# Layer two's features in another order, and four gathered quads instead of one ahead of the score block

## What is computed

```python
Qh = (x @ Wq + bq).reshape(N, 8, 32); Kh = (x @ Wk + bk)...; Vh = (x @ Wv + bv)...
s = jnp.einsum('nhc,nhc->nh', Qh, Kh) / jnp.sqrt(32.)      # one score a node and head
alpha = jax.nn.leaky_relu(s[src] + s[dst], 0.2)
m = jax.ops.segment_max(alpha, dst, num_segments=N)
e = jnp.exp(alpha - m[dst])
attn = jax.ops.segment_sum(Vh[src] * (e / denom[dst])[:, :, None], dst, num_segments=N)
```

## Time and profile before

| | |
|---|---|
| median of 3 runs | 2749.72 us (2741.72 to 2752.97) |
| the profiled execution's own time | 2740.57 us |
| its span | 2738.8 us |
| PE, DVE, ACT, POOL busy | 61%, 60%, 30%, 53% |
| mean granted clock of PE | 0.802 of full speed |

### The profile page before, as it was taken

How to read it: one execution, slowest core, us unless ns; L and a number is a source line. 1 busy time by engine, 2 the same in 40 slices (tenths; PEclk the granted TensorE clock), 3 DMA queues, 4 the chain that set the end, 5 groups by cost and what they waited for, 6 DMA issues and landing times. The chain is left out here.

```text
span 2738.8 us, 38544 instructions
## 1 busy us (share of the span) xinstructions
PE 1679.5 (61%) x9983; PEld 1342.2 (49%) x9983; DVE 1652.3 (60%) x2687; ACT 833.9 (30%) x2134; POOL 1444.6 (53%) x1557
## 2 busy tenths in 40 slices
PE   4367534677655544486655777504477767767688
PEld 4255423455543433486544566403355545545577
DVE  6455763677654545676424655796366657668675
ACT  3144210000000000465212222205355545534454
POOL 3655676655656664526155555477665655530050
PEclk8599857788876776588777999856689888878899
DMA  4535544555423333344152545454555555331010
GB/s 137 183 101 159 178 140 123 170 174 157 120 81 92 95 92 106 112 142 131 51 175 81 163 154 160 161 190 128 157 166 170 172 164 158 106 101 32 4 43 31
DMA packets 132988, 346.47 MB, mean 127 GB/s; under 512 B 39881, under 2 KB 66521, under 8 KB 119347
## 3 DMA queue, kind: packets, MB, share of 16 engines
q0 software_dynamic: 66144, 180.94, 23.5%
q1 hardware_dynamic: 63407, 158.51, 16.5%
q10 hardware_dynamic: 3364, 6.16, 0.7%
HBM read 262.24 MB, written 83.28 MB: 126 GB/s over the span
## 5 line engine op out<-in xcount | busy, mean ns | idle before, releaser
L1366 PE MATMUL ms_ps_m<-ms_msg,ms_pick 128*128 128x260 f32 x1408 | 415.6, 458 | 287.1 <-issue 199.8
L892 POOL DMA_INDIRECT e_ring<-table,e_index x465 | 442.6, 952 | 252.2 <-issue 137.6
L1347 DVE TENSOR_TENSOR ms_msg<-e_ring,ms_ps_w 128x1040 f32<-128x1040 f32 (+1 forms) x352 | 436.6, 1240 | 141.8 <-issue 128.0
L1366 PEld LDWEIGHTS ms_ps_m<-ms_msg,ms_pick 128*128 128x128 f32 x1408 | 313.0, 229 | 389.7 <-issue 332.2
L1366 PE MATMUL ms_ps_m<-ms_msg,all_xn 128*128 128x272 f32 x1408 | 386.0, 437 | 191.5 <-issue 167.1
L892 POOL DMA_INDIRECT e_ring<-table,l_index x369 | 353.9, 959 | 227.3 <-issue 111.1
L1366 PEld LDWEIGHTS ms_ps_m<-ms_msg,all_xn 128*128 128x128 f32 x1408 | 290.0, 212 | 287.3 <-issue 218.9
L767 PE MATMUL sc_ps_e<-sc_keys,sc_hot 125*128 125x100 bf16 (+1 forms) x3840 | 322.7, 241 | 168.6 <-DVE all_xn L712 141.7
L767 PEld LDWEIGHTS sc_ps_e<-sc_keys,sc_hot 125*128 125x128 bf16 x3840 | 276.8, 104 | 238.8 <-issue 123.4
L934 POOL DMA_INDIRECT w_staged<-table,l_stage_index x256 | 257.3, 1005 | 183.5 <-issue 66.9
L670 ACT ACTIVATE sc_rows<-sc_ps_b 125x512 bf16<-125x512 f32 x320 | 171.2, 598 | 433.6 <-PE sc_ps_b L755 251.8
(11 more groups left out here) (513 smaller groups left out, 2743.3 us busy)
## 6 DMA issues: line engine op xcount, KB each, us to landing
ahead<-w_staged SPq DMA_DIRECT2D x32, 1056.0 KB
e_ring<-ahead SPq DMA_DIRECT2D x32, 1056.0 KB
ahead<-e_ring SPq DMA_DIRECT2D x20, 1040.0 KB
e_ring<-ahead SPq DMA_DIRECT2D x20, 1040.0 KB
e_ring<-table,e_index POOLq DMA_INDIRECT x465
all_acc<-ahead SPq DMA_DIRECT2D x27, 256.0 KB
ahead<-all_acc SPq DMA_DIRECT2D x27, 256.0 KB
e_ring<-table,l_index POOLq DMA_INDIRECT x369
```

The source lines that it names most:

```text
L892: pool.indirect_dma_start(out=g.ring[:, slot * QUAD + i // GT, i % GT, :], out_offset=None, in_=s.table[:, :], in_offset=bass.IndirectOffs ...
L1347: dve.tensor_tensor(msg[:, b, :, 0:R].rearrange("p t (h o) -> p t h o", h=H), ring[:, bass.ds(slot, 1), :, :].rearrange("p a t (h o) -> p ...
L1366: mm = pe.matmul(ps_m[b][:, 0:W], pick[:, b, t, :], msg[:, b, t, :], start=t == 0, stop=t == GT - 1)
```

## The change

`BEGUN` becomes STAGES, so POOL gathers all four quads of the first round, 32 gathers, at the end of the features' block. And the features are written in another order on PE, ACT and DVE: the values of all five blocks come before the queries and keys of blocks 1 to 4.

```diff
-    BEGUN = 1
+    BEGUN = STAGES
...
                 turn_rows(0)
                 turn_rows(1)
                 values(0)
+                turn_rows(2)
                 values(1)
+                values(2)
                 queries_and_keys(0)
-                turn_rows(2)
-                values(2)
-                queries_and_keys(1)
-                node_scores(0)
                 turn_rows(3)
                 values(3)
-                queries_and_keys(2)
-                node_scores(1)
                 turn_rows(4)
                 values(4)
-                queries_and_keys(3)
-                node_scores(2)
-                queries_and_keys(4)
-                node_scores(3)
-                node_scores(4)
+                for b in range(1, NB):
+                    queries_and_keys(b)
+                    node_scores(b - 1)
+                node_scores(NB - 1)
...
                 highs(1)
+                highs(2)
+                second_norm(3)
                 queries(0)
-                highs(2)
-                queries(1)
-                second_norm(3)
                 highs(3)
                 second_norm(4)
-                queries(2)
                 highs(4)
-                queries(3)
-                queries(4)
+                for b in range(1, NB):
+                    queries(b)
...
+                norm(1)
                 lows(0)
-                norm(1)
                 norm(2)
                 lows(1)
                 dve.wait_ge(ones_set, 1)
                 values(0)
                 values(1)
-                products(0)
                 lows(2)
-                values(2)
                 combine(3)
                 norm(3)
-                products(1)
-                keep_scores(0)
+                values(2)
+                products(0)
                 combine(4)
                 norm(4)
                 lows(3)
                 values(3)
-                products(2)
-                keep_scores(1)
                 lows(4)
                 values(4)
-                products(3)
-                keep_scores(2)
-                products(4)
-                keep_scores(3)
-                keep_scores(4)
+                products(1)
+                for b in range(NB):
+                    keep_scores(b)
+                    if b + 2 < NB:
+                        products(b + 2)
```

## The result

| | before | after |
|---|---|---|
| median (7 runs each) | 2749.72 us | 2779.72 us (2762.64 to 2789.55) |
| ratio, 95% interval | | 1.0107 (1.0073 to 1.0142) |
| the profiled execution | 2740.57 us | 2762.64 us |
| its span | 2738.8 us | 2760.9 us |
| POOL's first gather to the last score kept | 15.5 us | 60.9 us |

The stages add up: 39.2 + 5.2 - 22.6 + 1.9 - 1.5 = 22.2 us, the difference of the spans. About 6.5 of the 39.2 are older than the edit: the first value of the features is kept at 1321.08, at 1314.59 before.

The account below looks back on a forecast made before the run. No engine is busy over 61%, so waits bind, with 40.7 us lost around the score block's start. Boundary +8 and score block -24 sum to -16: 2749.7 - 16 = 2733.7 us, range 2714 to 2760.

Parts of the forecast that it names:

- Part 1, the order: Features: with values ahead of queries and keys, the last values come 12 us earlier, bounds 0 and 14.8 us.
- the 4 us for PE's lower clock level: Features: 4 us added to the hand-made chain of values for PE's lower clock level after its pauses.
- Part 2, POOL and the boundary (+8): End of the features: 30 us of gathers, less 10 of idle and 12 of earlier start, move the boundary +8 us.
- POOL has some 10 us to spare there: Ahead of the boundary: POOL's 10.56 us of idle after the first quad counted as room for gathers.
- stays within 3 us of 1392: End of the features: PE's total work is unchanged, so the last score hardly moves and doesn't hold the boundary.
- The second rival: Stops move into the features: 26 us, 8 hidden behind POOL's end, boundary 18 us later, 2751 us; chance 0.20.
- The first quad's 10 us run beside the same work cost under 2 us: Features: argument against stops moving there, from the one quad gathered beside the same work before.
- The stores at the boundary: Boundary: SP's four stores begin together beside the first loads of sc_pair; costed at 0, bound 3 us.
- Part 3, the score block (-24): Start of the score block: 16.5 us remain of 40.7 lost, a gain of 24 us, bounds 0 and 38.
- Part 4, the rest (0): From item 5 on: POOL is paced by the lookups, its head start buys nothing, all behind moves equally.
- 0.66 us per us of run: Score block: loss charged per us of POOL's unbroken indirect transfers, from 40.7 us lost over 61.5 us of runs.
- my counterexample: Weights' stage: in a 93 us run of POOL, PE's result of 1782.48 reaches DVE at 1782.79, without delay.

Follow-up runs that it names:

- e2: The changed kernel with one quad instead of four gathered ahead of the boundary, the new order of the features kept; ratio 1.0032.
- e6: The changed kernel with SP's four stores started only when the first two pair loads have landed; ratio 0.9977.
- long jobs: The three jobs in which the kernel before had a median of 2745 to 2758 us, as in the first measurement.
- short jobs: The three jobs in which the kernel before had a median of 2313 to 2316 us and no engine stood behind POOL's runs.
- f2: The kernel before with POOL waiting for one more item after every second scatter and, from the 20th on, per four gathers; ratio 1.0037.
- f3: The changed kernel with quads paced by products, scatters paced by two and SP's stores behind the first pair loads; ratio 0.9957.
- h1: The changed kernel with direct transfers of fixed rows in place of the staged quads' gathers, in one of the long jobs; ratio 0.9273.
- g2: The changed kernel, unedited, measured a third time, in one of the short jobs; ratio 1.0046.
- f1: The changed kernel, unedited, measured again in one of the long jobs; ratio 0.9971.
- e3: The changed kernel with memsets on POOL in place of 21 of the 24 gathers of quads 1 to 3 ahead of the boundary; ratio 0.9963.
- g1: The changed kernel with direct transfers of fixed rows in place of the staged quads' gathers, in one of the short jobs; ratio 0.9693.

## Why the prediction was wrong

I forecast -16 us; the profiles give +22, and 2779.7 lies above the range's 2760.

*Part 1, the order:* right. From the first value kept to the last, 1321.08 to 1365.46 is 44.4 us, where it was 1314.59 to 1371.70, 57.1: 12.7 us less, and I had said 12. All profiles agree: 42.6 to 45.7 us in the new order, 57.1 to 59.2 in the old. No row priced the 4 us for PE's lower clock level in that sum. The new order by itself leaves the last score where it was, too: 76.8 us behind the first value in e2, 77.3 before.

*Part 2, POOL and the boundary (+8):* **the step that failed**, twice over. First, "POOL has some 10 us to spare there": it had not. The 10.56 us of idle in the earlier trace rows were mostly the close of its block, which ends 8.4 to 10.2 us after the start of the last gather in every kernel here; in the kernel before it ran until 1393.65, 3.0 us ahead of the first work behind the boundary (1396.69), and where it is what binds, that distance is 1.2. So the slack was 1.8 us. I took a wait that the view named after SP for slack. With the close counted, part 2 is about +17, not +8: in the changed kernel POOL's close ended at 1419.27 and alone would have put the boundary at 1420.5. Second, the last score "stays within 3 us of 1392. It doesn't bind": it was kept at 1431.1 and it was what bound. The second rival named this mechanism, at 26 us of stops and 0.20. It was 60.9 - 26.9 = 34 us. I had 8 us of it hidden behind POOL's end; since the close is longer, some 18 were, and 1435.9 - 1420.5 = 15.4 us showed at the boundary. "The first quad's 10 us run beside the same work cost under 2 us" was true (e2: 0) and misled me: eight gathers in a row cost 0, 16 cost 12, 32 cost 29 to 34.

The stores at the boundary, "I cost it at 0, the bound is 3 us": the first reduction came 5.2 us later than before, and holding the stores back gives 9 (e6). The bound rested on a wrong reading: POOL's first transfer behind the boundary takes 2.49 us in e6 too, at 1191.60, when the first store is issued only at 1196.59. Its 2.42 us in the earlier trace rows say nothing of the store.

*Part 3, the score block (-24):* right in size: 22.6 us from the first reduction to the eleventh, 34.3 left of 56.9. The distance of the eleventh from the boundary was 56.5 us, between the "about 50" and the "over 60" that I had given.

*Part 4, the rest (0):* right in the long jobs, where 64 gathers are left to POOL behind the lookups with one quad ahead as with four, and the part behind them took 983.7 and 982.2 us.

*From -16 to +22:* 9.3 for the close (17.3 instead of 8), 15.4 for the stops behind it, 5.2 for the stores, 1.4 for part 3 (22.6 of 24), 0.4 behind the eleventh reduction, and 6.5 that are older than the edit: 38.2 us.

The reason behind part 3 was too narrow. I priced the stops at 0.66 us per us of run over a steady pace of 1.91 us a step and took that pace for PE's. In the short jobs it is 1.37 (204.0 / 149): the steady pace holds stops too. Over 218 us, the lookups lose 0.55 to 0.67 us for each of 177 to 194 indirect transfers in ten profiles, paced or not (before 123 / 194 = 0.64, after 102 / 177 = 0.58, f2 0.62, f3 0.57). So it is nearer to a toll on each transfer than to a price of long runs, and a transfer moved from one place with dense exchange between PE, ACT and DVE to another takes its toll along. It is not one price: h1's 17 transfers, nearly back to back, cost 17 us (235.0 - 218), 1.0 each. In the features the 24 moved gathers put off the last score by 34 us, 1.4 each, and the boundary by as much (31.7 us behind the first gather in e2, 65.7 here); by g2's 50.2, some 18 of these would be there without any stop, as POOL's own run and close. Leaving the score block the gathers gave back about 21 (341.4 - 320.6). That is the change. The weights' stage, with few signals, pays nothing: from the last reduction to the first work on messages it is 124.3 us before and 124.2 in g2. That was my counterexample, and it was the place to look at.

How sure is the sign? The changed kernel gave 1.0107, 0.9971 and, in a short job, 1.0046. The two in long jobs exclude each other's intervals, so jobs differ by more than the interval says; I would say between no change and 1% slower, with no run that shows a gain clear of noise. In f1 the boundary came at 1421.7 instead of 1435.9, with POOL's start 9 us earlier, which the features' first value brought along, and 29 us of stops instead of 34: that is 14 of the 25.7 us between the two spans.

## What to carry to other kernels

Work that an engine has left over beside a chain of short exchanges need not be free for the chain, even if their busy times fit: price it by an experiment that leaves the engine busy and takes away the transfers (e3, h1). Before counting an idle stretch ahead of a block's end as slack, ask what closes the block. And where several stores are made ready at once, look at what loads stand beside them: one wait on SP gave 9 us at that place, in all six runs that had it (12.9 to 13.1 us to the first reduction).

## What the runs showed of the hardware

- In the long jobs PE's, ACT's and DVE's signals come late while POOL issues indirect transfers (gathers of 135 KB as well as scatters of 4 KB), PE's up to 29 us; not while it fills memory (e3), and not with direct transfers of the same bytes (h1). I can't say what is shared. The Trainium skill (SBUF — State Buffer, Who interferes with whom) has only the port pair of GpSimd and VectorE, which a fill uses and which cost nothing here; by it TensorE and ScalarE wait on no other engine, so the stops had nothing to do with POOL, and e3 and h1 say otherwise.
- It comes and goes with the job: on one chip the kernel before had a median of 2312.5 us in one job and 2745.4 in a later one, with POOL's instructions equally long (0.95 us) in both. What differs is open.
- A block whose last work on POOL is a transfer closes 8.4 to 10.2 us after that transfer's start, and the next block begins 1.2 us behind the close at the earliest. It is no matter of the indirect form: with direct ones it was 9.9 us (g1, h1), only there the last score came later and held the boundary.
